# First attention of a two-block transformer kernel: the eight pieces of the products with V are laid out one per place from 1 to 6 and two at place 7

## What is computed

```python
hn = _layernorm(x, ln1_g, ln1_b)
q = (hn @ wq + bq).reshape(b, s, NH, D).transpose(0, 2, 1, 3)     # 16 heads, D = 8
k = (hn @ wk + bk).reshape(b, s, NH, D).transpose(0, 2, 1, 3)
v = (hn @ wv + bv).reshape(b, s, NH, D).transpose(0, 2, 1, 3)
scores = jnp.einsum('bhqd,bhkd->bhqk', q, k) / jnp.sqrt(jnp.float32(D))
attn = jax.nn.softmax(scores, axis=-1)
o = jnp.einsum('bhqk,bhkd->bhqd', attn, v)
x = x + (o.transpose(0, 2, 1, 3).reshape(b, s, h) @ wo + bo)
```

## Time and profile before

| | |
|---|---|
| time, median of 3 runs (lowest to highest) | 2012.79 us (2010.74 to 2014.05) |
| the profiled execution's own time | 2014.68 us |
| its span, first to last instruction | 2013.0 us |
| the first attention in it | 331.9 to about 710 us |
| L1279, maxima on DVE: count, mean of one | 512, 683 ns |
| L1316, exponentials on ACT | 512, 600 ns |
| L1365 / L1378, score matmuls | 512 and 512, 409 and 388 ns |
| L1421, products with V | 2048 records, 383 ns |

### The profile page before, as it was taken

How to read it: one execution, slowest core, us unless ns; L and a number is a source line. 1 busy time by engine, 2 the same in 40 slices (tenths; PEclk the granted TensorE clock), 3 DMA queues, 4 the chain that set the end, 5 groups by cost and what they waited for, 6 DMA issues and landing times. The chain is left out here.

```text
span 2013.0 us, 48064 instructions
## 1 busy us (share of the span) xinstructions
PE 1752.2 (87%) x18438; PEld 760.4 (38%) x18438; DVE 1587.1 (79%) x2988; ACT 1286.2 (64%) x2656; POOL 1104.3 (55%) x712
## 2 busy tenths in 40 slices
PE   6537857999999955977999999999999999999997
PEld 3337832233333344653442333333333333333334
DVE  7843577999999575437779898999989899998963
ACT  4403243888888710216884777777787877787785
POOL 8713541000000055331135888989888998989895
PEclk9769977899999956988997999999999999999998
DMA  1230045111111061117994232332323223232311
GB/s 48 36 51 3 1 145 190 46 49 39 48 42 46 13 200 51 50 54 265 374 405 128 65 86 74 76 82 68 86 65 85 73 78 82 68 86 65 85 29 42
DMA packets 194487, 180.14 MB, mean 89 GB/s; under 512 B 58740, under 2 KB 155124, under 8 KB 194052
## 3 DMA queue, kind: packets, MB, share of 16 engines
q1 hardware_dynamic: 185860, 170.01, 29.0%
q0 software_dynamic: 2944, 7.10, 1.1%
q10 hardware_dynamic: 5504, 0.73, 0.2%
HBM read 101.16 MB, written 75.26 MB: 88 GB/s over the span
## 5 line engine op out<-in xcount | busy, mean ns | idle before, releaser
L975 DVE TENSOR_REDUCE maxima_l<-max_l 128x1 f32<-128x512 f32 x1024 | 644.5, 692 | 81.2 <-PE max_l L1077 81.2
L1037 ACT ACTIVATE probs_l<-exp_l 128x512 f32<-128x512 f32 x1024 | 575.3, 595 | 204.7 <-PE exp_l L1088 195.3
L951 POOL TENSOR_TENSOR part_sums_l<-probs_l 128x1024 f32<-128x1024 f32 x256 | 605.2, 2364 | 117.1 <-ACT probs_l L1037 106.8
L1077 PE MATMUL max_l<-k_stack_l,q_stack_l 96*128 96x512 f16 x1024 | 399.5, 391 | 4.0 <-DVE pv_bank_l L967 3.3
L1088 PE MATMUL exp_l<-q_stack_l,k_stack_l 100*128 100x512 f16 x1024 | 390.3, 382 | 5.3 <-ACT probs_l L1037 2.9
L1279 DVE TENSOR_REDUCE maxima_l<-max_l 128x1 f32<-128x512 f32 x512 | 317.1, 683 | 16.6 <-PE max_l L1365 16.5
L1316 ACT ACTIVATE probs_l<-exp_l 128x512 f32<-128x512 f32 x512 | 279.2, 600 | 58.3 <-PE exp_l L1378 54.6
L1122 PE MATMUL pv_bank_l<-probs_l,v_ring_l 128*32 128x512 f32 x2048 | 273.8, 606 | 14.9 <-ACT probs_l L1037 14.9
L1077 PEld LDWEIGHTS max_l<-k_stack_l,q_stack_l 96*128 96x128 f16 x1024 | 100.1, 98 | 328.3 <-DVE maxima_l L975 272.7
L1793 POOL IOTA rows_e<- 128x32 int32 x1 | 0.2, 183 | 384.6 <-POOLq L26 384.6
L957 POOL TENSOR_TENSOR part_sums_l<-part_sums_l 128x512 f32<-128x512 f32 x128 | 162.9, 1273 | 10.0
(11 more groups left out here) (294 smaller groups left out, 2435.4 us busy)
## 6 DMA issues: line engine op xcount, KB each, us to landing
scratch_qk_l<-parts_g SPq DMA_DIRECT2D x128, 256.0 KB, 9.1
q_stack_l<-scratch_qk_l SPq DMA_DIRECT2D x192, 128.0 KB
k_stack_l<-scratch_qk_l SPq DMA_DIRECT2D x192, 128.0 KB
scratch_v_l<-v_g SPq DMA_DIRECT2D x16, 1024.0 KB
v_ring_l<-scratch_v_l SPq DMA_DIRECT2D x64, 256.0 KB, 3.3
scratch_stack_l<-parts_c SPq DMA_DIRECT2D x16, 384.0 KB, 3.6
q_stack_l<-scratch_stack_l SPq DMA_DIRECT2D x64, 96.0 KB, 2.2
k_stack_l<-scratch_stack_l SPq DMA_DIRECT2D x64, 96.0 KB, 2.3
```

Of the source, the lines that this page charges most:

```text
L951: pool.tensor_tensor(part_sums[:, i, h, :, :], probs[:, i, h, 0:2, :], probs[:, i, h, 2:4, :], ALU.add).then_inc(pair_sum.sem, 1)
L975: dve.reduce_max(maxima[:, s % 2, at % NT, at // NT:at // NT + 1], max_bank(n, at)[:, :], AX).then_inc(max_taken.sem, 1)
L1037: act.activation(probs[:, i, at // NT, at % NT, :], exp_ps[at % 2][:, :], ACT.Exp, scale=a.scale).then_inc(prob_tile.sem, 1)
L1077: pe.matmul(max_bank(n, at)[:, :], qs[0:SHIFT_ROW, s % RING, h, k * P:(k + 1) * P], ks[0:SHIFT_ROW, s % RING, h, :], start=True, stop=True ...
```

## The change

The table of places is changed, and the wait for the exponentials is no longer one wait of piece 0 for all 16 tiles, but one wait of each of the pieces 0 to 3 for the last tile that it reads: 9, 11, 13 and 15.

```diff
-L0_VALUES_AT = (1, 1, 2, 3, 4, 5, 5, 6)
+L0_VALUES_AT = (1, 2, 3, 4, 5, 6, 7, 7)
@@ attention_l0, block.tensor
                         for piece in [piece for piece in range(2 * NT) if L0_VALUES_AT[piece] == p]:
+                            if piece < NT:
+                                pe.wait_ge(prob_tile.sem, prob_tile.made(m, TILES - HALVES * (NT - piece) + 1))
                             if piece == 0:
                                 pe.wait_ge(v_loaded[slot], nth(turn, s - PV_LAG, 16))
-                                pe.wait_ge(prob_tile.sem, prob_tile.made(m, TILES - 1))
                                 if exists(turn, s, OUT_LAG):
```

## The result

The changed kernel takes 2022.38 us (median of 6, 2020.22 to 2024.93) against 2012.68 for the kernel before (median of 6, 2010.74 to 2014.05, three of them those of the table ahead of the prediction): a ratio of 1.0051, 95% interval 1.0038 to 1.0063, +9.7 us. Ratios here leave out two disturbed executions, one of the kernel before (8841.77 us) and one of experiment 2 (2285.78 us at a mean granted clock of 0.72). Forecast were 2019.2 us, a range of 2013.5 to 2024 and a chance of 0.70 for slower.

The account below looks back on a forecast made before the run. The prediction took DVE to bound the stage, late wherever TensorE doubles pieces. Step 3 -0.8, steps 4 to 6 -0.4, step 7 +0.45, five batches +5.4, steps 28 to 31 and end: +6.4, giving 2019.2 us, range 2013.5 to 2024.

Parts of the forecast that it names:

- The bound: Whole stage: DVE sets the pace, and two pieces at one place cost it about a quarter microsecond.
- The gap rule: TensorE between places: 1.24 us without a stall; one piece makes 1.09, two make 1.52 and stall by 0.28.
- The waits are dead: Pieces 0 to 3: the 96 added waits are always fulfilled, release nothing and cost 0 us.
- Place 7 with OT and OUT: End of steps s = 3 and s = 0: two pieces add 0.87 behind OT and 0.98 behind OUT.
- rival 1: Stalls only change places; full 0.38 gain at place 1, OT and OUT overlap the pieces: +1.7, 2014.5 us; chance 0.14.
- Places 1 to 3: DVE's tiles 0 to 6: ACT is late next, so -0.15 us, not -0.38; +0.11 in s = 0, -0.06 in s = 1.
- Sum of the middle: Steps 4 to 6 -0.4 us, step 7 +0.45, five batches in steps 8 to 27 +5.4.
- The end: After DVE's last maxima: pieces behind OT and OUT of steps 31 and 32 +1.96, place 5 -0.2 twice: +1.55 us.
- The start: Step 3, the first with V, at half clock: one piece less, -0.8 us.
- rival 4: The clock rises later because step 3 has less to do: +2 us on top, 2021.3 us; chance 0.06.
- Rival 2: Place 7's pieces are hidden since place 0 has none: about -10 us, 2003 us; chance 0.08.

Follow-up runs that it names:

- experiment 2: The kernel before with the new places and its one old wait of piece 0; ratio to before 1.0047, a batch of 45.00 us.
- experiment 1: The kernel before with the new waits of pieces 0 to 3 alone, places as before; ratio to before 0.9999, a batch of 43.90 us.
- experiment 11: Changed kernel with pieces at places 0 to 6, ACT's copy behind exponential 13 of the same step, the one old wait; 2007.50 us, ratio to before 0.9973.
- experiment 6: The changed kernel with ACT's copy of the sums cut to the left 256 of 512 columns; a batch of 44.42 us.
- experiment 4: The kernel before and the changed kernel, both unchanged, run again for a second trace each; 2012.87 and 2015.94 us.
- experiment 5: The changed kernel with the old places in step 3 alone; 2016.01 us in one execution.
- experiment 7: The changed kernel with three pieces at place 7 and none at place 6; 2034.18 us in one execution, a batch of 46.72.
- experiment 9: The kernel before with the new places only in steps with s = 1 or 2 and a max pass; ratio to before 0.9999, a batch of 43.93 us.

## Why the prediction was right, and the term that was not

**The bound.** "The stage is bound by DVE, and each doubled place costs it about a quarter microsecond": shown. In the batch the clock, the work and DVE's rate stayed, only the brackets moved.

**The gap rule** (1.24 us from a place's second max matmul to the next place's first): shown by a dose. Two pieces at place 7 give D14 to D0 of 1.48, three give 1.92, for 1.20 without lateness. By the rule it would be 0.28 and 0.71 late; it was 0.28 and 0.72. In the kernel before a double at place 5 gives 0.27.

**The waits are dead:** shown by experiment 1, and experiment 11 shows the reason, since they live as soon as piece 0 moves ahead of exp matmul 3.

**Place 7 with OT and OUT:** forecast D0 +0.87 and +0.97; D14 to D0 went from 1.20 to 2.07 and from 1.59 to 2.57, +0.87 and +0.98. That they might overlap with the pieces (rival 1) fell with the 0.99 us of the trace and the unchanged 0.58 and 1.09 of OT and OUT themselves.

**Places 1 to 3:** forecast D0 to D6 of 3.83; it is 2.41 + 1.43 = 3.84. In s = 0 +0.11 was forecast and 4.32 - 4.22 = +0.10 came. That ACT is late next is shown by experiment 6. In s = 1 steps -0.06 was forecast and nothing came: D0 to D6 is 4.26 in both kernels.

**Sum of the middle.** Steps 4 to 27: -0.4 + 0.45 + 5.4 = +5.45 forecast, 268.00 - 262.64 = +5.36 measured. A batch in it, s = 0 to 3: +0.80, 0.00, -0.15 and +0.44, where +0.82, -0.04, -0.13 and +0.45 were forecast. Steps 28 to 31: +0.25 forecast, +0.22 measured.

**The end:** +1.55 forecast, +1.26 measured between the two traces without a stretch of half clock, 0.65 up to step 33's addition to the residual and 0.61 from there to the last. That is 0.13 to 0.17 less each time than the 0.98 - 0.2 of the forecast, whose 0.2 no row shows either. The stretch of half clock was not forecast. Eleven of the fourteen traces have one, the kernel before among them, so that it comes at all can't be shown to be an effect of the change. That it comes some 16 us earlier with the new places is one (experiment 4).

**The start was wrong.** The step "one piece less: -0.8" failed. It took the clock as given and priced the piece alone. Measured are 41.80 - 40.91 = +0.9 against the first trace, +0.6 against the second (41.19). The mechanism is rival 4's, which was given a chance of 0.06: with one piece instead of two at place 1 of step 3 the clock rises some 3 us later, and experiment 5 turns it back with that one step. Rival 4's price of +2 us on top of the forecast was near too; the error is 1.4 to 1.7 us of a forecast of +6.4.

**What the pieces add up to:** 0.6 to 0.9 at the start, 5.4 in steps 4 to 27, 0.2 in steps 28 to 31 and 1.3 to 1.6 at the end, 7.5 to 8.1 us. The second pair of traces gives 7.8 for the stage. The measured ratio's interval is 7.6 to 12.7 us, so the sum is at its lower end. Between the first two traces (10.3 us) the rest is the clock at the end. Whether the changed kernel meets the longer stretch more often stays open; one of its two traces had it. The forecast of +6.4 is thus 1.1 to 1.7 us short of what the pieces did. The measured median, +9.7, also lies inside the range, but the clock at the end, to which part of it may be due, was in no term: that much is luck.

Rival 2 (place 7 hidden because place 0 is empty) fell with the bracket at place 0 of every step, and with experiment 7 most plainly.

## What to carry to other kernels

Here a consumer that reads from a ring of three banks gave the producer a fixed allowance between two of its matmuls (1.24 us), and an empty place before it was not saved up. So read the longest gap, not the mean per place, and put extra work neither twice into one place nor beside other extra work. Before splitting a wait, look whether an instruction ahead of it in the same list already waits for more. Here it helped only together with a move ahead of that instruction (experiments 1 and 11), and the move first needed the buffer's release, ACT's copy, to come earlier.

## What the runs showed that I had not expected

- Taking matmuls *out* of a stretch at half clock made the stretch longer: the rise went from 33.1 to 33.8 us behind DVE's first maximum to 36.5 to 37.1, though TensorE's records fill the time in either case. The window in the changed kernel just before the rise:

```profile
364.00:368.80 4.80, 4.80 (x31) 0.74 (x29) 2.58 (x4) 2.45 (x6) 0.00 (x0) 0.50 0.02 5
```

- In the last steps, where TensorE waits for ACT, the clock fell for 3.4 us (once 6.9 us) in eleven of fourteen traces, in one of the two of the kernel before: worth 1.6 us in 30 (31.59 against 29.95), and 2.6 for the 6.9 us (33.77 against 31.21). The places set whether it falls in step 32 or in step 34.
- A late step is handed on through ACT: 0.28 us of lateness at place 0 (a bracket of 0.20) became 0.16 more at the next double place (experiment 9).
